# Expert layer: token rows gathered from DRAM and turned by a DMA transpose, in place of one-hot products

## What is computed

```python
def _L0_ffn_ref(x, gate_query, log_temp, w1, b1, w2, b2):   # x is layer-normed
    b, n, d = x.shape                                       # 128, 64, 128
    gate_logits = jnp.einsum('bnd,ed->ben', x, gate_query)  # 16 experts
    affinity = _sinkhorn(gate_logits / jnp.exp(log_temp))   # 6 iterations
    gates, idx = jax.lax.top_k(affinity, CAP)               # CAP = 32 of 64 tokens
    expert_in = jnp.take_along_axis(x[:, None, :, :], idx[..., None], axis=2)
    h = jax.nn.gelu(jnp.einsum('becd,edf->becf', expert_in, w1) + b1[None, :, None, :])
    expert_out = jnp.einsum('becf,efd->becd', h, w2) + b2[None, :, None, :]
    out = jnp.zeros_like(x)
    return out.at[jnp.arange(b)[:, None, None], idx].add(gates[..., None] * expert_out)
```

## Time and profile before

| | |
|---|---|
| runs of the kernel before, us | 1919.36, 1921.75, 1922.48 |
| median | 1921.75 |
| profiled execution: span from first to last instruction | 1918.0 |
| profiled execution's own time | not recorded apart from the span; the median is 3.75 above the span |
| TensorE busy | 1812.8 us (95%) |
| VectorE busy | 1609.1 us (84%) |
| ScalarE busy | 1564.4 us (82%) |
| GpSimd busy | 662.4 us (35%) |
| DMA packets | 312954, 160.67 MB |

### The profile page before, as it was taken

One profiled execution on the slowest core, in us unless ns is written; L12 is line 12 of the kernel. 1 busy time (PEld: TensorE's weight loads), 2 busy tenths in 40 slices (PEclk: granted clock), 3 DMA queues, 4 the chain that ended last, 5 costly groups with the idle time before them and its releaser, 6 DMA issues. The chain is left out here.

```text
span 1918.0 us, 72744 instructions
## 1 busy us (share of the span) xinstructions
PE 1812.8 (95%) x28635; PEld 1311.9 (68%) x28635; DVE 1609.1 (84%) x3645; ACT 1564.4 (82%) x2773; POOL 662.4 (35%) x918
## 2 busy tenths in 40 slices
PE   6999998896999999999999999998999999999898
PEld 4777776542666666666666666766777777777677
DVE  5999987598788888888888888778999999988744
ACT  5899997575998989898989989876888888888543
POOL 4788887231000000000000000004666666655565
PEclk8999999897999999999999999999999999999899
DMA  7644545495000000000000001004665555533233
GB/s 180 130 99 93 103 94 102 139 364 187 14 11 15 13 14 11 15 13 15 10 14 14 13 12 52 2 2 107 153 169 154 144 156 147 154 69 72 64 111 121
DMA packets 312954, 160.67 MB, mean 84 GB/s; under 512 B 236558, under 2 KB 295862, under 8 KB 312374
## 3 DMA queue, kind: packets, MB, share of 16 engines
q1 hardware_dynamic: 312278, 157.95, 31.4%
q10 hardware_dynamic: 480, 0.05, 0.0%
HBM read 62.33 MB, written 36.83 MB: 52 GB/s over the span
## 5 line engine op out<-in xcount | busy, mean ns | idle before, releaser
L1793 DVE TENSOR_TENSOR h<-g,h 128x1024 f16<-128x1024 f32 x256 | 313.3, 1224 | 138.3 <-ACT h L1725 138.0
L239 PEld LDWEIGHTS psE<-ew,h 128*128 128x128 f16 x6144 | 351.2, 98 | 56.0 <-issue 40.1
L239 PE MATMUL psE<-ew,h 128*128 128x128 f16 x6144 | 365.2, 219 | 12.8 <-DVE eo L1803 6.0
L1720 ACT ACTIVATE g<-psH,eb1T 128x512 f32<-128x512 f32 x512 | 330.2, 680 | 30.9 <-PE psH L239 24.5
L814 POOL TENSOR_TENSOR Ph<-E,Ph 128x512 f16<-128x512 f32 x192 | 222.0, 1156 | 235.9 <-ACT Ph L768 235.9
L1866 POOL MEMSET rbias<- 64x384 f32 x1 | 0.4, 411 | 839.2 <-POOLq L133 839.2
L1725 ACT ACTIVATE h<-g 128x1024 f16<-128x1024 f32 x256 | 270.6, 1057 | 8.1
L720 ACT ACTIVATE vB<-psV 128x512 f16<-128x512 f32 x384 | 225.9, 589 | 51.2 <-PE psV L618 49.0
L841 DVE TENSOR_TENSOR vB<-psV,vB 128x512 f16<-128x512 f32 x384 | 248.4, 678 | 1.1 <-ACT vB L720 1.0
L618 PE MATMUL psV<-shared 96*64 96x512 f16 x1536 | 209.9, 379 | 1.5 <-DVE vB L841 1.5
L820 POOL TENSOR_TENSOR E<-E,rden 128x512 f32<-128x512 f32 x192 | 199.7, 1040 | 15.1 <-DVE rden L852 14.3
(11 more groups left out here) (308 smaller groups left out, 3417.9 us busy)
## 6 DMA issues: line engine op xcount, KB each, us to landing
keys_ahead<-shared SPq DMA_DIRECT2D x52, 512.0 KB, 4.8
shared<-keys_ahead SPq DMA_DIRECT2D x52, 512.0 KB, 3.6
rawe<-in_L_ffn_w_dram SPq DMA_DIRECT2D x32, 256.0 KB, 3.1
wb<-rw SPq DMA_DIRECT2D x64, 128.0 KB, 2.0
rows<-places SPq DMA_DIRECT2D x110, 64.0 KB, 2.5
out_dram<-x SPq DMA_DIRECT2D x7, 512.0 KB, 3.2
context_T<-shared SPq DMA_DIRECT2D x64, 48.0 KB, 2.4
PT<-Ph SPq DMA_TRANSPOSE x192, 2.8
```

Of the source, the lines that this page charges most:

```text
L239: last = e.matmul(to, a, b, start=start and n == 0, stop=stop and n == 2, **flags)
L1720: e.activation(g32[:, ft, :], psH[:, ft, :], ACT.Gelu_apprx_tanh, bias=b1T[:, a.expert(1) * FT + ft:a.expert(1) * FT + ft + 1]).then_inc(s ...
L1793: e.tensor_tensor(h[:, 1 - par, 1, 2 * q:2 * q + 2, :], g32[:, 2 * q:2 * q + 2, :], h[:, 1 - par, 0, 2 * q:2 * q + 2, :], ALU.subtract)\
```

## The change

The one-hot gathering goes. Normalised tokens are written to DRAM as f16 rows (high half, low half: 512 bytes a token), one tensor for each group of 16 batches (`tokens16`). GpSimd prepares and stores the first 16 tiles during selection; the other 48 are made in the expert stage in every other step, as before, and SyncE stores each.

For each step GpSimd issues four indirect DMAs, each fetching 128 rows of 512 bytes by row numbers `row_slot` (`tok_slot` plus a base, one more VectorE instruction at the end of selection), into a ring of four buffers (`rows`). SyncE then issues one DMA transpose of 128x1024 f16 into a ring of three (`xg`), after the gather has landed and the first layer of step n-3 is done. TensorE waits for that transpose.

`psR`, `pick`, `sel`, `rows16`, `idx16`, `places` and both large `xg` buffers disappear; `psE` gets a second buffer, so the second layer of step n waits for the gating of step n-2 and no longer of n-1. The start-up loop of group 0 disappears. The gelu, the halves, `put`, the scatter products and the residual stay.

```diff
@@ constants @@
+GB = 16
+NGROUPS = B // GB
+SOON_TILES = 16
-    token_of_p = sb(whole, "token_of_p", [P, 1], F32)
+    slot_base = sb(whole, "slot_base", [P, B // 4], F32)
-    places = nc.dram_tensor("places", [B, NE * CAP], F16).ap()
+    tokens16 = [nc.dram_tensor(f"tokens16_{n}", [GB * N, 2 * D], F16).ap() for n in range(NGROUPS)]
@@ select_tokens, gpsimd @@
-                    e.wait_ge(s["it"], Z_READ)
-                    for t in range(8):
+                    for t in range(SOON_TILES):
                         if t >= 4:
                             e.wait_ge(s["rows_lo"], t - 3)
                         e.tensor_scalar(exact[:, t % 4, :], x[:, t, :], mean[:, t:t + 1], rstd[:, t:t + 1],
                                         ALU.subtract, ALU.mult).then_inc(s["rows"], 1)
...
+                        if t % GT == GT - 1:
+                            e.wait_ge(s["rows_lo"], t + 1)
+                            e.dma_start(tokens16[t // GT].rearrange("(t p) k -> p t k", p=P),
+                                        tiles16[:].rearrange("p t h d -> p t (h d)")).then_inc(s["tokens"], 16)
@@ select_tokens, vector @@
-                    e.wait_ge(s["idx"], NE // 4)
-                    e.tensor_copy(idx16[:], idx32[:].rearrange("p e c -> p (e c)")).then_inc(s["idx16"], 1)
                     e.wait_ge(s["slots"], 1)
-                    e.tensor_copy(gate_slot[:], psG[:])
-                    e.tensor_scalar(tok_slot[:], psI[:], block_of_p[:], None, ALU.add)
+                    e.wait_ge(s["tokens"], 16 * (SOON_TILES // GT))
+                    e.tensor_scalar(tok_slot, psI[:], block_of_p[:], None, ALU.add).then_inc(s["tok_slot"], 1)
+                    e.tensor_copy(gate_slot, psG[:])
+                    e.wait_ge(s["tok_slot"], 1)
+                    e.tensor_tensor(row_slot, tok_slot, slot_base[:].unsqueeze(1).broadcast_to([P, NE, B // 4]),
+                                    ALU.add)
@@ run_experts @@
+        GATHERED, TURNED = 4, 3
-            psE = ps(c, "psE", [P, RT, D], F32)
+            psE = ps(c, "psE", [P, 2, RT, D], F32)
-            psR = ps(c, "psR", [P, 512], F32)
@@ run_experts, sync @@
+                    def transpose(n):
+                        a = Expert(n)
+                        wait(e, s[f"rows{a.gathered}"], turn(n, GATHERED), 16 * RT)
+                        wait(e, s["H"], at(n - TURNED), FT)
+                        e.dma_start_transpose(xg[:, a.turned], rows[:, a.gathered]).then_inc(s[f"xg{a.turned}"], 16)
+
+                    def store_tile(t):
+                        k = t - SOON_TILES
+                        wait(e, s["x_lo"], at(k))
+                        e.dma_start(tokens_of_tile(t), xn[:, k % 2].rearrange("p h d -> p (h d)"))\
+                         .then_inc(s[f"kept{k % 2}"], 16)
...
+                    for n in range(STEPS):
+                        transpose(n)
+                        if n == 0:
+                            e.wait_ge(s["shares"], 64)
+                            load_shares(0)
+                        if n % NE == 8 and n // NE + 1 < NG:
+                            load_shares(n // NE + 1)
+                        t = made_tile(n - 4)
+                        if t is not None:
+                            store_tile(t)
+                        if n == STEPS - 2 * NE:
+                            load_all(e, s["next"], [
...
@@ run_experts, gpsimd: new @@
+                    def gather(n):
+                        a = Expert(n)
+                        if a.e == 0 and a.G * GT >= SOON_TILES:
+                            for par in range(2):
+                                e.wait_ge(s[f"kept{par}"], 16 * (a.G * GT + GT - SOON_TILES) // 2)
+                        if n >= GATHERED:
+                            before = n - GATHERED
+                            e.wait_ge(s[f"xg{before % TURNED}"], 16 * (before // TURNED + 1))
+                        for r in range(RT):
+                            at_rows = bass.IndirectOffsetOnAxis(ap=row_slot[:, a.e, RT * a.G + r:RT * a.G + r + 1], axis=0)
+                            e.indirect_dma_start(out=rows[:, a.gathered, 2 * D * r:2 * D * r + 2 * D], out_offset=None,
+                                                 in_=tokens16[a.G], in_offset=at_rows)\
+                             .then_inc(s[f"rows{a.gathered}"], 16)
+
+                    for n in range(STEPS):
+                        gather(n)
@@ run_experts, tensor @@
-                            take(tpar, a.bp, (psR[:], psH[:, 3, :]))
+                    def first_layer(a):
+                        wait(e, s[f"xg{a.turned}"], turn(a.n, TURNED), 16)
+                        for ft in range(FT):
+                            wait(e, s["gelu"], at(a.n - 1), FT, ft + 1 - FT)
...
+                    def second_layer(a):
+                        wait(e, s["h_lo"], a.j, 2)
+                        wait(e, s["gated"], at(a.n - 2))
@@ run_experts, scalar @@
-                            e.activation(rows_of(a)[1], psH[:, 3, :].rearrange("p (e c) -> p e c", c=CAP), ACT.Copy)\
-                             .then_inc(s["g_1"], 1)
@@ run_experts, vector @@
-                            gathered_rows(a.t, a.bp, rows_of(a)[0], psR[:])
...
-                            select(a.t + 1, (a.k + 1) % 2, False)
```

More of the change, by code:

```diff
@@ L1677, in _ @@
-                    all_steps(e, body)
+                    def first_layer(a):
+                        wait(e, s[f"xg{a.turned}"], turn(a.n, TURNED), 16)
+                        for ft in range(FT):
+                            wait(e, s["gelu"], at(a.n - 1), FT, ft + 1 - FT)
+                            last = matmul3(e, psH[:, ft, :], [w1[:, hl, a.e, ft * P:ft * P + P] for hl in range(2)],
+                                           [a.rows(hl) for hl in range(2)])
+                            last.then_inc(s["H"], 1)
@@ new lines, in biases @@
+                    def biases(G):
+                        wait(e, seeded["xadd"], at(G - 1))
+                        wait(e, s["weigh"], at(G), 96)
+                        for r in range(RT):
+                            for bp in range(2):
+                                side = slice(64 * bp, 64 * bp + 3 * NE)
+                                last = e.matmul(psA[:, bp, r, :], weigh[side, r, :], b2[side], start=r == 0, stop=False,
+                                                skip_group_check=True)
+                        last.then_inc(s["bias"], 1)
@@ new lines, in scatter @@
+                    def scatter(a):
+                        wait(e, s["put"], a.j, RT)
+                        wait(e, s["eo_lo"], a.j)
+                        if a.e == 0:
+                            biases(a.G)
+                        for r in range(RT):
+                            for hl in range(2):
+                                for bp in range(2):
+                                    side = slice(64 * bp, 64 * bp + 64)
+                                    last = e.matmul(psA[:, bp, r, :], put[side, r, :], eo[side, hl, r, :], start=False,
+                                                    stop=a.e == NE - 1 and hl == 1, skip_group_check=True)
+                        last.then_inc(s["A"], 1)
@@ new lines, in puts, with low @@
+                    def puts(a):
+                        wait(e, seeded["A"], at(a.n - 1))
+                        for r in range(RT):
+                            e.tensor_scalar(put[:, r, :], iota[:], tok_slot[:, a.e, a.G * RT + r:a.G * RT + r + 1],
+                                            None, ALU.is_equal).then_inc(s["put"], 1)
+                    def low(a):
+                        wait(e, s["eo_hi"], a.j)
+                        e.tensor_tensor(eo[:, 1], eo32[:], eo[:, 0], ALU.subtract).then_inc(s["eo_lo"], 1)
```

464 lines of the change are left out of this document (155 added, 309 removed).

## The result

The changed kernel takes **2102.24 us** (median of 4 runs, 2100.24 to 2105.25) against 1920.72 for the kernel before (median of 4 runs, the three listed ahead of the prediction and a fourth): ratio **1.0945**, 95% interval 1.0929 to 1.0961. It is slower by 9.5%; forecast were 1872.5 us and a range of 1863 to 1950. The profiled execution has a span of 2100.9 us.

The account below looks back on a forecast made before the run. TensorE was taken to set the pace throughout the expert stage. Steps -42.6, start -6.5, selection +1.3 and end -1.5 sum to -49.3 us, giving 1872.5 us from a median of 1921.75; range 1863 to 1950.

Parts of the forecast that it names:

- The steps: Expert stage: 112 gathering steps fall from 6.37 to 5.99 us each, -42.6 us.
- The cost of nothing for the tiles' halves: Expert steps: normalisation, f16 half and subtraction, kept every other step, fit into idle time of ScalarE and VectorE; costed at nothing.
- The stall of the earlier trace: First layers: TensorE waits for a PSUM bank ScalarE empties late; rival that it stays: 17.4 us back, 1890, chance 0.09.
- The start: Opening of the expert stage: first layer at 469.5 instead of 476.01, -6.5 us.
- Before the stage: Selection: POOL prepares 16 tiles instead of 8 beside VectorE's critical normalisation, +1.3 us.
- The end: Last second layer: with two psE buffers it starts at 1286.3 instead of 1287.92, -1.5 us.
- Feeding the steps: Expert stage: POOL needs 4.6 us of each 5.99 us step, so it keeps up; transposes and transfers stay hidden.
- c: POOL's issue time for one indirect DMA: taken as 1.16 us, bounded by 0.44 and 2.37.
- the rival with a chance of 0.06: VectorE's comparisons and normalisations hold up POOL's descriptors, 1.2 us a step; 1978 us at an issue time of 1.40; chance 0.06.
- The comparisons I had blamed: Expert steps: VectorE's four f16 comparisons, 4 x 0.25 us, during which POOL might not work at its descriptors.
- the point from which GpSimd leads: Expert stage: up to 1.50 us an indirect DMA TensorE still leads; from 1.59 the stage ends later than now.
- The last group is thus a sample of what the kernel does once the one-hot products are gone: Expert stage: the last 15 steps, which gather nothing, at 5.99 us each, stand for every step after the change.

Follow-up runs that it names:

- e18: Changed kernel plus 257 long-over waits behind GpSimd's last gather, loaded and timed anew: 1872.82 us, ratio 0.9756 to the kernel before.
- e1: Changed kernel without its 512 indirect DMAs (row buffers hold a constant), transposes kept: 1868.26 us.
- e4: Changed kernel with plain DMAs of the same size, fixed rows, same queue, in place of the indirect ones: 1865.29 us.
- e15: Changed kernel, all 512 indirect DMAs kept, plus a tiny plain DMA from GpSimd's queue every second step: 1908.16 us.
- e7: Changed kernel with two of the four fetches of each step plain, alternating with indirect ones: 1868.23 us.
- e9: Changed kernel issuing only three of the four indirect DMAs of each step, the missing rows holding a constant: 1872.18 us.
- e13: Changed kernel with indirect fetches in steps 0 to 63 and plain ones in steps 64 to 127: 1868.42 us.
- e16: Changed kernel with one expert in eight fetched plainly, plus 129 long-over waits behind the last gather: 1871.51 us.
- e5: Changed kernel with every indirect DMA fetching rows 0 to 127 in order instead of the selected rows: 2083.64 us.

## Why the prediction was wrong, step by step

I go through the sum first by e18, which does the changed kernel's work without the standing, and then come to what failed in the changed kernel itself.

**The steps**, without the standing, are as forecast: -42.6 us. In e18 the first first layer starts at 472.16 and the last at 1233.57, 761.4 us, against 1279.03 - 476.00 = 803.0: -41.6. The cost of nothing for the tiles' halves holds: 671.81 / 112 = 6.00 us a step (e1 without any gather: 5.97). The stall of the earlier trace rows is gone, so that rival falls.

**The start:** -6.5 forecast, with +1.3 for the selection ahead of it -5.2; measured 472.16 - 476.01 = -3.9 for both. e18 from there:

```profile
458.35 0.85 DVE L1402 TENSOR_TENSOR of_slots<-of_slots,slot_base 128x512 uint32<-128x512 f32 x1
...
460.98 1.09 POOL L1580 DMA_INDIRECT scratch<-tokens,of_slots  x1 [2.33 <-POOLq L136]
462.38 0.96 POOL L1580 DMA_INDIRECT scratch<-tokens,of_slots  x1 [0.30 <-issue]
...
467.45 1.27 SPq L1535 DMA_TRANSPOSE scratch<-scratch  x1
...
472.17 4.99 PE L247 MATMUL psH<-scratch,ew 128*128 128x512 f16 x12 [15.13 <-DMA scratch<-scratch]
```

The stage opens at 460.98 (forecast 460.1: VectorE's copy of 0.68 us now stands in front of the addition too). The fourth DMA is issued at 465.83 and landed by 467.45, 1.6 after (2.0 forecast). The transpose takes 4.7 us to TensorE's start where I took the attention's 2.8; that term is the one that was mis-sized most. **Before the stage** one trace of before can't settle the +1.3. The last MAX8 of the selection starts at 453.43 us there and at 453.94 to 455.86, median 454.46, in the 18 traces with the changed selection (455.16 in the changed kernel itself, 453.94 in e18), so something like it came. The instruction of the earlier trace rows at 457.18 starts at 457.08 in e18 all the same, because it no longer stands behind the copy of the gates. **The end** is right: from the last first layer to the last second layer 8.89 us before (1287.92 - 1279.03) and 1240.93 - 1233.57 = 7.36 in e18, -1.5. Together -47.2 in the span (1918.0 to 1870.8) against -49.3. That e18's 1872.82 us is so near to 1872.5 is partly luck: those 2.1 us are made up for by the 3.75 between span and median, which is 2.0 in e18 (1872.82 - 1870.8).

**Feeding the steps** had a cost wrong, though it didn't make the kernel slow: c. GpSimd needs 0.94 us and 0.30 between two, 1.24 where I took 1.16. On top of that VectorE does hold it up, the rival with a chance of 0.06, only by another instruction than I named. VectorE beside the DMAs above, in e18:

```profile
479.00 1.23 DVE L1696 TENSOR_TENSOR h<-g,h 128x1024 f16<-128x1024 f32 x1 [1.02 <-ACT h L1667]
479.10 1.95 POOL L1580 DMA_INDIRECT scratch<-tokens,of_slots  x1 [0.30 <-issue]
...
481.25 1.23 DVE L1696 TENSOR_TENSOR h<-g,h 128x1024 f16<-128x1024 f32 x1 [1.02 <-ACT h L1667]
481.35 1.94 POOL L1580 DMA_INDIRECT scratch<-tokens,of_slots  x1 [0.30 <-issue]
...
483.49 1.23 DVE L1696 TENSOR_TENSOR h<-g,h 128x1024 f16<-128x1024 f32 x1 [1.02 <-ACT h L1667]
483.60 1.94 POOL L1580 DMA_INDIRECT scratch<-tokens,of_slots  x1 [0.30 <-issue]
```

A DMA that begins inside such a subtraction, which reads two tiles of SBUF, ends 0.81 us behind it (480.23 + 0.81 = 481.04), however long it had to wait, or behind the next subtraction (7 of 247); one in which a subtraction begins later takes its 0.94. The comparisons I had blamed cost next to nothing: 30 of the 512 DMAs end 0.81 us behind one, at most 0.07 us late. Plain DMAs from GpSimd are not held: of e4's 512, 202 begin inside this subtraction and the longest of them takes 0.55 us. Over the stage 47% of the DMAs end 0.81 us behind this subtraction, the mean is 1171 ns, and the pitch (1215.5 - 461.0) / 511 = 1.476 us: 5.91 a step, of TensorE's 5.93. The forecast put the point from which GpSimd leads at 1.50 and the one from which the gain is gone at 1.59. So GpSimd is 0.02 us a DMA short of leading and 0.11 short of eating the gain; e15 shows the other side of it, where 0.3 us more a step on GpSimd made it the bound and cost 35 us. The section that the prediction cites, the Trainium skill's SBUF — State Buffer, "SBUF: two separate sides", names beside the two-port mode a VectorE instruction with two SBUF inputs: of it and a GpSimd instruction that reads SBUF one waits for the other. With that the rows agree in kind: the subtraction has two SBUF inputs, an indirect DMA takes its row numbers from SBUF, a plain one none. The loss is at most 1.02 us for a DMA (1956 ns against 940).

**The step that failed** is the cost of a step, and with it the sentence "The last group is thus a sample of what the kernel does once the one-hot products are gone". It put a step at 5.99 us; in the changed kernel it takes 7.93, and the stage from the first first layer to the last takes 993.1 us, 190.1 more than before where 42.6 less were forecast. I took for granted, without writing it down, that an engine which waits for nothing gets its next instruction at once. TensorE set the pace in both stretches before, and it doesn't in the changed kernel, while no engine and no queue there is full: the runs show the standing in its place, and its cause is open. All my rivals were waits of the program or full engines; none was an engine that stands for no reason in the program, and a case of this kind lay far outside the range. I could not have priced it from the trace of before, which has no indirect DMA; but a new kind of operation, 512 times, deserved a wider end on the slow side than c alone gave.

## What to carry to other kernels

When a changed kernel is slow and every engine has idle time, read what the idle time is put down to before anything else: "issue" in the middle of a row of matmuls that wait for nothing isn't a dependence and isn't an engine at its limit. Then vary what should not matter before believing a cause: here one theory fell with e7, the next with e9, and three more with e13, e15 and e16, and with dead waits behind the last gather the kernel took 229 us less. And when gathering through GpSimd, count 1.24 us for an indirect DMA of up to 128 rows plus what VectorE's instructions with two operands in SBUF hold it up, and compare that with the step.

## What I had not expected of the hardware

- TensorE, ScalarE and VectorE stand between instructions that wait for nothing (33 us in one second layer of 2.84) in six kernels with 512 indirect DMAs and in none with 448 or fewer. Two more with 512 don't stand: the changed kernel with 257 dead waits behind it, and with 64 tiny plain DMAs between.
- An indirect DMA costs GpSimd 0.94 us for 128 rows and 0.90 for 64, with 0.30 between two; in order or scattered makes no difference (e5: 0.948 median). A plain one of the same bytes costs 0.54.
- An indirect DMA that begins while VectorE subtracts two SBUF tiles ends 0.81 us behind the subtraction, up to 1.96 us long in place of 0.94 (e18). A plain one isn't held (e4, 0.55 us at most).
- GpSimd issued 512 of them in 755 us with 1.2 us of waiting (e18), and TensorE beside them was busy 99% of its time.
